# A tower of embedding, attention and experts: the last set of tokens is normalised and turned inside the attention's first pass

## The reference, cut to what matters

```python
raw = weight[indices]                      # gather 4096 rows of 192
h = fake_quantize_tcfp12(raw)              # blocks of 64: int8 main part and NF4 residual
x = (h - mean(h)) / sqrt(var(h) + 1e-5)    # layer norm without weights
q, k, v = x @ W_Q + b_Q, x @ W_K + b_K, x @ W_V + b_V          # 12 heads of 64
z = softmax(mask(q k^T / 8)) v
h = h + z @ W_O + b_O
h = h + ssinf3(layernorm(h), ...)          # experts
```

## Time and profile before

| what | before |
|---|---|
| median of 3 runs | 2627.59 us (2624.28 to 2630.31) |
| the profiled execution, its own time | 2633.09 us |
| its span, first to last instruction | 2631.4 us |
| busy PE / DVE / ACT / POOL | 90% / 71% / 47% / 47% |
| mean granted clock of TensorE | 0.963 |

### The profile page before, as it was taken

The page is one execution under the profiler, slowest core; times in us unless marked ns, Lnnn a source line. Parts: engine busy times, 40 slices in busy tenths (PEclk is TensorE's granted clock), DMA queues, the critical chain, the costliest instruction groups (busy, mean ns, idle before and its releaser), DMA issues. The chain is left out here.

```text
span 2631.4 us, 42687 instructions
## 1 busy us (share of the span) xinstructions
PE 2369.2 (90%) x16192; PEld 1254.9 (48%) x16192; DVE 1876.9 (71%) x3802; ACT 1245.0 (47%) x1760; POOL 1245.7 (47%) x858
## 2 busy tenths in 40 slices
PE   3564899999999999999999999986999999999998
PEld 1233556665656565656565665543333333333332
DVE  7864665756565756656565656687988888988987
ACT  3322233333333333333333333345777777787776
POOL 5000265767675757675766666653413413323120
PEclk9786999999999999999999999996999999999999
DMA  1002000000001000000000001132011001000000
GB/s 50 12 15 62 1 8 7 3 10 1 9 1 33 1 10 1 10 1 9 1 10 1 10 1 20 19 52 56 9 19 27 9 19 21 15 19 17 11 7 7
DMA packets 42941, 39.35 MB, mean 15 GB/s; under 512 B 26865, under 2 KB 35186, under 8 KB 41842
## 3 DMA queue, kind: packets, MB, share of 16 engines
q1 hardware_dynamic: 40608, 31.18, 5.4%
q0 software_dynamic: 1536, 3.15, 0.4%
q10 hardware_dynamic: 594, 2.31, 0.2%
HBM read 26.13 MB, written 10.49 MB: 14 GB/s over the span
## 5 line engine op out<-in xcount | busy, mean ns | idle before, releaser
L690 POOL TENSOR_TENSOR acc<-acc,pT 128x1024 f32<-128x1024 f32 (+3 forms) x412 | 837.9, 2034 | 228.5 <-ACT pT L1131 191.6
L1131 ACT ACTIVATE pT<-banks 128x1024 f32<-128x1024 f32 x480 | 406.8, 896 | 803.9 <-PE banks L769 758.3
L1868 DVE TENSOR_TENSOR hw<-hid,banks 128x512 f32<-128x512 f32 x1024 | 662.8, 680 | 86.4 <-PE banks L1551 71.9
L930 DVE TENSOR_REDUCE part<-banks 128x2 f32<-128x1024 f32 (+3 forms) x432 | 438.3, 1044 | 300.5 <-PE banks L745 298.6
L1710 ACT ACTIVATE hid<-banks 128x1024 f32<-128x1024 f32 x512 | 496.6, 1022 | 186.4 <-PE banks L1541 169.6
L785 PE MATMUL banks<-pT,v 128*64 128x512 f32 (+3 forms) x1920 | 405.7, 543 | 0.9 <-POOL pT L674 0.9
L1551 PE MATMUL banks<-wT,select 64*128 64x512 f16 x1024 | 342.8, 394 | 41.1 <-DVE hw L1868 21.4
L1541 PE MATMUL banks<-zst,w1c 50*128 50x512 f32 x1024 | 307.7, 545 | 12.7 <-ACT hid L1710 12.7
L1551 PEld LDWEIGHTS banks<-wT,select 64*128 64x128 f16 x1024 | 93.9, 94 | 398.5 <-DVE hw L1868 338.8
L1559 PE MATMUL banks<-hw,w 128*32 128x512 f32 x2048 | 278.3, 616 | 0.8 <-DVE hw L1868 0.8
L785 PEld LDWEIGHTS banks<-pT,v 128*64 128x64 f32 x1920 | 116.6, 136 | 194.6 <-issue 172.5
(11 more groups left out here) (243 smaller groups left out, 3239.5 us busy)
## 6 DMA issues: line engine op xcount, KB each, us to landing
zst<-z_scratch SPq DMA_DIRECT2D x48, 128.0 KB, 4.1
z_scratch<-zp SPq DMA_DIRECT2D x8, 512.0 KB, 2.8
out_h<-o SPq DMA_DIRECT2D x8, 384.0 KB, 2.6
xT_scratch<-xs_hi SPq DMA_DIRECT2D x4, 512.0 KB, 2.7
xt_hi<-xT_scratch SPq DMA_DIRECT2D x2, 1024.0 KB, 5.8
w<-in_L_ffn_W ACTq DMA_DIRECT2D x1, 2048.0 KB, 8.7
xt_hi<-in_L_ffn_W SPq DMA_DIRECT2D x12, 128.0 KB, 4.7
v<-in_L_ffn_W SPq DMA_DIRECT2D x12, 128.0 KB, 4.3
```

Source lines behind the costliest of these rows:

```text
L690: pool.tensor_tensor(acc[:, G % 2, :, off:CH], acc[:, G % 2, :, off:CH], pT[:, slot, :, 0:w], ALU.add).then_inc(summed, 1)
L930: last = dve.tensor_reduce(to[:, :, c:c + 1], both[:, :, 0:whole], AX.X, ALU.max)
L1131: act.activation(pT[:, J % PSLOTS, :, 0:CH - off], both[:, :, 0:CH - off], ACT.Exp, scale=E ** -0.5)\
L1868: dve.tensor_tensor(hw[:, n % 2, q, :], hid[:, n % 2, q, :], ring_bank(("w", g, n, q)), ALU.mult).then_inc(mixed, 1)
```

## The change

- The last set (p = 3) is quantised in the embedding as before, up to `levels`, but its squares, root, scalings, turn and store now lie in the attention's first pass: ACT does the 8 squares at item 6, DVE the variance at item 11 and the six small operations at item 13, ACT then the 8 scalings, PE the 16 transposes as two new items 20 and 21 of the ring ("xt"), which ACT copies out; SyncE stores them before it looks at the second pair's weights.
- In the embedding SyncE loads the first pair's weights and W_O behind the store of set 0, and the first batch's x behind the store of set 1. Nothing of these is loaded at the attention's start.
- PE starts a set when DVE has read the sums in PSUM (`levels_read`, behind L253), not when the means are there (behind L257).
- The turn of set 2, which lay behind the 14th gate of set 3, lies behind all of set 3.
- `level`, `xn` and the turned copy now live in the attention's `pT`; ACT waits for the store of the last set (`x_stored`) before the first exponentials write there, and SyncE before the second batch's x is loaded.

```diff
@@ embedding, SyncE
-            for p in range(NS):
+            for p in range(NS - 1):
                 sp.wait_ge(xT_copied, p + 1)
                 cols = slice(p * TS * P, (p + 1) * TS * P)
+                sp.dma_start(xT_dram[0:P, cols], xs_hi).then_inc(xT_stored, 16)
+                sp.dma_start(xT_dram[P:D, cols], xs_lo).then_inc(xT_stored, 16)
+                if p == 0:
+                    load_weights(sp, 0)
+                    for n in range(2):
+                        load_wo(sp, n)
+                if (p + 1) * TS * P == T:
+                    sp.wait_ge(xT_stored, 32 * (p + 1))
+                    load_x(sp, 0)
+            sp.wait_ge(xT_stored, 32 * (NS - 1))
@@ embedding, VectorE, levels(p)
-                link(dve.scalar_tensor_tensor(blocks(L), blocks(gate_sums), SCALE * NF4[0], per_block(rmax),
-                                              ALU.add, ALU.mult))
+                dve.scalar_tensor_tensor(blocks(L), blocks(gate_sums), SCALE * NF4[0], per_block(rmax),
+                                         ALU.add, ALU.mult).then_inc(levels_read, 1)
+                dve.wait_ge(levels_read, p + 1)
...
-            ln_variance(NS - 1)
-            ln_root(NS - 1)
@@ embedding, ScalarE
-            ln_square(NS - 1)
-            ln_scale(NS - 1)
-            take_x(NS - 1)
@@ embedding, TensorE
                 if p:
-                    pe.wait_ge(neg2_ready, p)
+                    pe.wait_ge(levels_read, p)
...
-                    if p and j == 13:
+                    if 0 < p < NS - 1 and j == 13:
                         turn(p - 1)
...
-            turn(NS - 1)
+            turn(NS - 2)
@@ attention
+        SQUARES_AT, VARIANCE_AT, SHIFT_AT, TURN_AT = 6, 11, 13, 20
...
+            if n == 0:
+                items[TURN_AT:TURN_AT] = [("xt", 0), ("xt", 1)]
@@ attention, SyncE
-            load_x(0)
-            load_weights(0)
-            for n in range(2):
-                load_wo(n)
+            sp.wait_ge(x_copied, 2)
+            sp.dma_start(xT_dram[0:P, B * T - TS * P:B * T], xs_hi).then_inc(x_stored, 16)
+            sp.dma_start(xT_dram[P:D, B * T - TS * P:B * T], xs_lo).then_inc(x_stored, 16)
@@ attention, TensorE
+            def turn_last(k):
+                banks = slot_free(place[("xt", k)])
+                pe.wait_ge(scaled, TS)
+                d0, d1 = ((0, P), (P, D))[k]
+                for t in range(TS):
+                    last = pe.transpose(banks[t // TQ][0:d1 - d0, (t % TQ) * P:(t % TQ + 1) * P],
+                                        xn[:, t * D + d0:t * D + d1], ident[:, :])
+                last.then_inc(filled, 1)
@@ attention, VectorE
+            def last_variance():
+                dve.wait_ge(squared, 1)
+                dve.tensor_scalar(lvar, lvar, 1.0 / D, LNEPS, ALU.mult, ALU.add).then_inc(variance_ready, 1)
+
+            def last_shift():
+                dve.wait_ge(rooted, 1)
+                link(dve.reciprocal(rstd_x, rstd_x))
+                link(dve.tensor_tensor(newton_x, rstd_x, rstd_x, ALU.mult))
...
+                dve.tensor_tensor(shift, neg2, rstd_x, ALU.mult).then_inc(shifted, 1)
...
-            for item in first_pass(0):
+            for m, item in enumerate(first_pass(0)):
+                if m == VARIANCE_AT:
+                    last_variance()
+                if m == SHIFT_AT:
+                    last_shift()
                 side(item)
@@ attention, ScalarE
+            def normalise_last():
+
+                for t in range(TS):
+                    at = slice(t * D, (t + 1) * D)
+                    last = act.activation(xn[:, at], level[:, at], ACT.Square, bias=neg2[:, t:t + 1],
+                                          accum_out=lvar[:, t:t + 1])
+                last.then_inc(squared, 1)
+                act.wait_ge(variance_ready, 1)
+                act.activation(rstd_x, lvar, ACT.Sqrt).then_inc(rooted, 1)
+                act.wait_ge(squared, 1)
+                act.wait_ge(shifted, 1)
+                for t in range(TS):
+                    at = slice(t * D, (t + 1) * D)
+                    act.activation(xn[:, at], level[:, at], ACT.Identity, bias=shift[:, t:t + 1],
+                                   scale=rstd_x[:, t:t + 1]).then_inc(scaled, 1)
+
+            def take_last(k):
+                both = item_in(("xt", k))
+                to = (xs_hi, xs_lo)[k].rearrange("p (g t) -> p g t", g=2)
+                act.activation(to, both[0:(P, DLO)[k], :, :], ACT.Copy).then_inc(x_copied, 1)
...
-            for item in first_pass(0):
+            for m, item in enumerate(first_pass(0)):
+                if m == SQUARES_AT:
+                    normalise_last()
                 side(item)
             split_w_high(1)
+            act.wait_ge(x_stored, 32)
```

More of the change, by code:

```diff
@@ L23 @@
 NT = B * T // P
+TS = NT // 4
 GT = 4
@@ L75, in tower, with sb_early, load_x, load_weights @@
         zst = sb("zst", [P, 2, NQ, GTOK], F32R)
+        early = ctx.enter_context(ExitStack())
+        def sb_early(name, shape):
+            return early.enter_context(nc.sbuf_tensor(name, shape, F32))
+        xt_hi, xt_lo = sb_early("xt_hi", [P, T]), sb_early("xt_lo", [P, T // 2])
+        w_hi, w_lo = sb_early("w_hi", [P, 3, P]), sb_early("w_lo", [P, 3, P])
+        bq, bk, bv_bc = sb_early("bq", [P, 2]), sb_early("bk", [P, 2]), sb_early("bv_bc", [P, 2, P])
+        wo = sb_early("wo", [P, 2, D])
+        x_in, w_in = ctx.enter_context(nc.semaphore("x_in")), ctx.enter_context(nc.semaphore("w_in"))
+        wo_in = [ctx.enter_context(nc.semaphore(name)) for name in ("wo_in_a", "wo_in_b")]
+        pT = sb_early("pT", [P, 6, 2, 512])
+        last_small = sb_early("last_small", [P, 6, TS])
+        def load_x(sp, b):
+            sp.dma_start(xt_hi[:, :], xT_dram[0:P, b * T:(b + 1) * T]).then_inc(x_in, 16)
+            for half in range(2):
+                sp.dma_start(xt_lo[half * DLO:(half + 1) * DLO, :],
+                             xT_dram[P:D, b * T + half * (T // 2):b * T + (half + 1) * (T // 2)])\
+                  .then_inc(x_in, 16)
+        def load_weights(sp, n):
+            p, u = n % NP, n % 2
+            for k, w in enumerate((w_q, w_k, w_v)):
+                wd = w.rearrange("h d e -> d h e")
+                for dst, d0 in ((w_hi[:, k, :], 0), (w_lo[0:DLO, k, :], P), (w_lo[DLO:P, k, :], P)):
+                    sp.dma_start(dst.rearrange("d (h e) -> d h e", e=E),
+                                 wd[d0:d0 + dst.shape[0], 2 * p:2 * p + 2, :]).then_inc(w_in, 16)
+            for dst, src in ((bq, b_q), (bk, b_k)):
+                sp.dma_start(dst[:, u:u + 1], src.rearrange("h (e a) -> (h e) a", a=1)[p * P:(p + 1) * P, :])\
+                  .then_inc(w_in, 16)
+            sp.dma_start(bv_bc[:, u, :], b_v.rearrange("(a g) e -> a (g e)", g=2)[p:p + 1, :]
+                         .to_broadcast([P, P])).then_inc(w_in, 16)
+        def load_wo(sp, n):
+            p = n % NP
+            sp.dma_start(wo[:, n % 2, :], w_o.rearrange("h e d -> (h e) d")[p * P:(p + 1) * P, :])\
+              .then_inc(wo_in[n % 2], 16)
         z_dram = nc.dram_tensor("z_scratch", (2, P, GTOK), F32, kind="Internal").ap()
@@ L125, in stage_embed @@
         blk = sb("blk", [P, 11, NBS])
-        small = sb("small", [P, 6, TS])
         amax, total, neg, var, s, r, t, scale, s127 = (blk[:, i, :] for i in range(9))
         rmaxes = [blk[:, 9 + i, :] for i in range(2)]
-        total2, neg2, lvar, rstd, newton, shift = (small[:, i, :] for i in range(6))
+        total2, neg2, lvar, rstd, newton, shift = (last_small[:, i, :] for i in range(6))
         idx_in, bias_in, rows_in = sem("idx_in"), sem("bias_in"), [sem(f"rows_in_{i}") for i in range(2 * NS)]
@@ L343, in take_x @@
                     act.wait_ge(xT_stored, 32 * p)
-                act.activation(xs_hi[:, :], turned_hi, ACT.Copy)
-                act.activation(xs_lo[:, :], turned_lo, ACT.Copy).then_inc(xT_copied, 1)
+                act.activation(xs_hi, turned_hi, ACT.Copy)
+                act.activation(xs_lo, turned_lo, ACT.Copy).then_inc(xT_copied, 1)
             square(0)
@@ L462, in stage_attention @@
         w1, cm = w1c[:, :, 0:M * HID], w1c[:, :, M * HID:]
+        level, xn, xs_hi, xs_lo = last_tokens(pT)
+        _, neg2, lvar, rstd_x, newton_x, shift = (last_small[:, i, :] for i in range(6))
         mask_ready, consts_ready = sem("mask_ready"), sem("consts_ready")
-        x_in = sem("x_in")
-        w_in, wo_in = sem("w_in"), [sem("wo_in_a"), sem("wo_in_b")]
         filled = sem("ring_filled")
         x_high, x_low, w_high, w_low = sem("x_high"), sem("x_low"), sem("w_high"), sem("w_low")
+        squared, variance_ready, rooted, shifted = (sem("last_squared"), sem("last_variance"), sem("last_rooted"),
+                                                    sem("last_shifted"))
+        scaled, x_copied, x_stored = sem("last_scaled"), sem("last_copied"), sem("last_stored")
         hi_done, low_taken, v_taken = sem("hi_done"), sem("low_taken"), sem("v_taken")
@@ L831, in side @@
```

(4 more changed lines are left out.)

72 lines of the change are left out of this document (25 added, 47 removed).

## The result

The changed kernel takes 2609.15 us, the median of four runs (2606.61 to 2610.01), beside 2626.09 us of the kernel before in four runs (2624.28 to 2630.31): 16.9 us less by the medians. The ratio on record is 0.9919, with an interval of 0.9906 to 0.9933, which is 17.6 to 24.7 us. The medians alone give 0.9935, just outside that interval; the record does not say how its ratio is formed, so the gain is known only as some 17 to 21 us. Forecast were 2607.8 us and 19.8 us less.

A forecast was written before the change was run, and what follows sets the result against it. TensorE was taken to bound the kernel from 303 us on, DVE the first pass before it. The terms -17.9 - 12.0 + 4.4 + 5.7 = -19.8 us against 2627.6 gave 2607.8 us, range 2599 to 2617.

The forecast's parts named there:

- Set 3's early start and the moved turn: Embedding, set 3: levels at 191.0 instead of 195.41, 4.4 us sooner, 2.6 from the start and 1.8 from the turn.
- The block's end: Embedding's end: last set's normalising leaves the chain, next block begins at 199.0, not 216.87; -17.9 us.
- The loads: Attention's start: the first loads, issued early behind stores of sets 0 and 1, no longer delay ACT's split; -12.0 us.
- The middle sets: Sets 1 and 2: early start wins nothing, idle TensorE loses its clock ahead of the gates; +4.4 us (0 to 5.8).
- The first rival: Sets 1 and 2: the clock is not lost over the gap; -24.2 us, 2603.4 us, chance 0.20.
- the one on the other side: Sets 1 and 2: the clock does not come back after the gap; +15.0 us, 2642.6 us, chance 0.03.
- The first pass: Attention's first pass: the inserted work of the last set costs +5.7 us, ends 0.6 and 12.6.
- the hole at item 15: First pass: item 15 waits for item 12's copy, which stands behind ACT's 8 scalings; +4.2 us.
- item 22's: First pass: DVE has nothing behind item 19 until PE fills item 22, since 20 and 21 are not its work; +1.0 us.
- The table: Attention's first pass: the moved Sqrt runs under the table already loaded, so nothing is counted for a load.
- Its rival: First pass: the moved Sqrt needs its own table load between variance and shift; +1.3 us, 2609.1 us, chance 0.05.
- The slower and the eaten-up rival: Clock stays low in sets 1 and 2 (2642.6 us, chance 0.03); saved seam eaten elsewhere (within 5.3 of 2627.6, chance 0.04).

The follow-up runs named there:

- e1: The changed kernel run again without an edit, as the measure for the others; 2609.93 us, ratio 0.9919.
- e2: Changed kernel with the old wait (for the means) again in sets 1 and 2, the finer wait kept in set 3; 2603.43 us, ratio 0.9897.
- e10: Changed kernel with old wait in sets 1 and 2, scalings behind item 12's copy, and store's wait ahead of the split; 2600.96 us, ratio 0.9894.
- e8: Changed kernel with the last set normalised, turned and stored in the embedding again; 2618.84 us, ratio 0.9963.
- e7: Changed kernel with x, weights and W_O of the first pass loaded at the attention's start again; 2619.62 us, ratio 0.9968.
- e3: Changed kernel with the residual's matmuls done twice in sets 1 and 2, the first time for nothing; 2605.88 us, ratio 0.9906.
- e4: Changed kernel with ACT's scalings of the last set behind item 12's copy, not in front of it; 2604.79 us, ratio 0.9903.
- e5: Changed kernel with the old wait (for the means) in all sets; 2606.22 us, ratio 0.9916.
- e12: e10 with the residual's matmuls also done twice in set 3, the first time for nothing; 2601.43 us, ratio 0.9897.

## Why the prediction was right

**What bounds it.** What changes ahead of the loop moves it as one block: e1 has 2317.6 us from the handover to the end of its span, the kernel before 2317.8. Over all kernels this stretch varies between 2314.7 and 2318.3 us (2315.2 in the changed kernel's first profile) with no order in the edits; the forecast counts nothing there and need not.

**Set 3's early start and the moved turn.** Forecast: first gate matmul at 171.4, 90 in 19.6 us, levels at 191.0 if nothing else moved. e2 has 171.58, but 21.24 us; e10 171.33 and 19.60. The two middle sets put 3.9 us in front (2.6 + 1.3), and the changed kernel has its levels at 195.20, so 191.3 without them. Right. "Set 3 has a gap of only 1 us and keeps its clock" held in the changed kernel (1.24 us, 19.60) and e1, but not always: in e2 the clock rose early in L423 (0.96 from 168.0 us on) and ended it sooner, the gap was 2.11 us, and the matmuls behind lost 1.6 us; e8 had the same (2.12 us, 21.23).

**The block's end.** Forecast 199.0 + 4.4 = 203.4 for SyncE's next block; ACT's split came at 203.12. Store to next block 203.12 - 198.89 = 4.2 us, as read.

**The loads.** -12.0 forecast; e7 measured 10.9 by the medians and 11.5 in the trace.

**The middle sets.** +4.4 forecast, 0 to 5.8 as bounds. Seven profiles have a gap of 4.5 to 5.8 us in both sets: the 84 matmuls take 19.59 to 21.27 us, 20.47 on the mean of the fourteen, 2.17 us above 18.30 where 2.2 were forecast. e2 took the cause away and e3 did so in another way. The first rival (the clock is not lost) falls; so does the one on the other side, since the clock came back each time.

**The first pass.** +5.7 forecast, 0.6 to 12.6 as bounds. From split to split it is 4.8 us longer (57.0 to 61.8): the hole at item 15 was named with its cause and sized 4.2 (item 15 begins 36.5 us behind the split, it was 32.8: 3.7), item 22's with 1.0 (1.06 idle). Behind item 15 the rest took 25.3 us where it took 24.2, and item 22's hole is all of that: the 0.5 us added for a fallen clock did not show, and item 15 came 0.5 us sooner than sized. SyncE's second weights cost nothing, as forecast: they were issued up to 255.6 and wanted at 264.9. (Their sum in the prediction is 286.3, not 286.6, which changes nothing.) e4 confirms the cause. What the forecast did not have is the stretch from the second split to the handover, where 2.7 us came back (27.5 to 24.8; 25.3 in e1). The kernel before has the stretched DVE operation and the fallen clock there, the changed kernel neither: from the first split to the handover it is 84.55 us before and 86.58 after, only 2.0 more.

**The table.** No load of its own for the moved Sqrt: the groups show the same number of loads after. Its rival falls. The Trainium skill's "ScalarE activation tables: per-element evaluation and per-set limits" (Table sets in the compiler and the runtime) says only that loads are placed block by block. The prediction read this as a load for each block that might need one; the trace has none here. The load for the exponentials moved behind a wait instead, which no row had told me.

**The sum.** -25.9 at the first split (forecast -25.5), -21.1 at the second (forecast -19.8), -23.9 at the handover and -23.0 in e1, against -16.9 and -19.8 by the medians. The traces show more because of the execution of before that was profiled: it took 2633.09 us, 7.0 above the median of its four runs and 3.3 above that of the nine beside e1. Profile against profile the gain is 26.5 us, and 23.2 in e1, and the forecast of 19.8 is 3.4 to 6.7 us too small; the handover's 2.7 us are the largest known part of that. Set against the median of before, the same 19.8 gave 2607.8, and 2609.15 was measured. So the mechanisms and most of the sizes were right, but that the total agrees to 1.4 us is partly luck. The stated range, 2599 to 2617, is the sum of the bounds moved up by 1 us, for which no reason is given.

**The slower and the eaten-up rival** have nothing for them in any of the profiles: the clock came back in every set, and nothing took back the seam.

## What to carry to other kernels

Starting an engine earlier is worth nothing when its second instruction waits for something that does not move; if the engine is TensorE, the gap that the early start opens can cost the clock of what comes behind, as it did here, so a wait should be made finer only where the work behind it can follow at once. Work that is put into a ring of items must be placed, on each engine, behind the copies that free the ring: 3.6 us of ACT's scalings in front of one 0.6 us copy cost 3.8 us of the bounding engine, one place later they left no idle time there. And a wait that a change adds can hold back a table load that stands in front of the next instruction.

## What the runs showed of the hardware that I had not expected

- The clock after a gap: with 4.5 to 5.8 us of idle TensorE it fell in all fourteen sets; with 2.73 us in e3's set 1, 2.11 us in e2's set 3 and 2.12 in e8's it fell too; with 1.85 us and less ahead of the gates (e3, e5, e10, e12) it stayed. No threshold follows: at the end of the first pass it fell after a wait of 1.90 to 1.93 us in four profiles and stayed in two. In e2 the row of the granted clock is 0.50 just behind the gap:

```profile
169.50:171.30 1.80, 0.00 (x0) 0.00 (x0) 1.77 (x2) 1.80 (x9) 0.00 (x0) 1.00 0.01 5
171.70:174.40 2.70, 2.70 (x7) 0.91 (x7) 2.70 (x4) 0.82 (x4) 0.00 (x0) 0.50 0.00 0
```

  What a gap costs varies: after one of 4.55 us the 84 matmuls took 1.3 us more in e7 and 3.0 us more in e1. Why is not shown.
- A DVE operation on 128 x 8 numbers takes 0.17 us alone and 0.95 us when GpSimd's copy of 128 x 1024 started 0.11 us ahead of it; it ends just behind the copy (272.60 and 272.57). The Trainium skill's "SBUF — State Buffer" (Who interferes with whom) says that the two engines share a pair of ports under an exclusive lock, and that a VectorE instruction with two inputs in SBUF contends with a GpSimd instruction that reads SBUF. This operation has two such inputs, `negmax` and `cpad`, and the copy reads `pT`; the trace agrees.
- The table load waits with the instruction that it stands before. Where ACT had a wait of its own between the split and the first exponential, the load came 12.56 us of idleness later than it could have (278.18); with the wait moved ahead of the split it came at once (266.74).
